# Rotated projection in eight products per chunk instead of twelve, with the two halves added by VectorE

## The reference, cut to what matters

```
ct_q  = x @ Wd_q_w + Wd_q_b
query = heads(ct_q @ Wu_q_w + Wu_q_b) + heads(rope(ct_q @ Wq_r_w + Wq_r_b))
ct_kv = x @ Wd_kv_w + Wd_kv_b
key   = heads(ct_kv @ Wu_k_w + Wu_k_b) + heads(rope(x @ Wk_r_w + Wk_r_b))
value = heads(ct_kv @ Wu_v_w + Wu_v_b)
```

## Time and profile before

| | |
|---|---|
| median of 3 runs | 3408.21 us |
| lowest and highest | 3405.76 and 3410.78 us |
| the profiled execution | 3409.91 us, its span 3408.1 us |
| projection, chunks 0 to 15 | from 69.94 us to about 687.6 us of the span |
| one chunk in the loop | 37.15 us |
| PE busy over the whole span | 94% |

### The profile page before, as it was taken

The page is one execution under the profiler, slowest core; times in us unless marked ns, Lnnn a source line. Parts: engine busy times, 40 slices in busy tenths (PEclk is TensorE's granted clock), DMA queues, the critical chain, the costliest instruction groups (busy, mean ns, idle before and its releaser), DMA issues. The chain is left out here.

```text
span 3408.1 us, 49590 instructions
## 1 busy us (share of the span) xinstructions
PE 3214.4 (94%) x16020; PEld 2024.3 (59%) x16020; DVE 2122.1 (62%) x2249; ACT 1538.2 (45%) x2714; POOL 2025.6 (59%) x654
## 2 busy tenths in 40 slices
PE   7999999989999999999999999999995999999998
PEld 4888888744444444444444444444442777877777
DVE  3545554756666666666666666666643778777774
ACT  1222221146666656566656666666663233232332
POOL 0111111157777777787777777877784566666653
PEclk8999999989999999999999999999997999999999
DMA  3544445544242423323242322324204223333230
GB/s 97 185 167 166 171 170 168 156 97 97 54 97 54 97 54 74 77 58 91 54 97 54 80 71 64 87 51 97 54 11 145 74 68 94 98 98 84 70 93 38
DMA packets 179890, 316.27 MB, mean 93 GB/s; under 512 B 16080, under 2 KB 52080, under 8 KB 179696
## 3 DMA queue, kind: packets, MB, share of 16 engines
q1 hardware_dynamic: 179696, 313.70, 33.4%
HBM read 194.59 MB, written 118.49 MB: 92 GB/s over the span
## 5 line engine op out<-in xcount | busy, mean ns | idle before, releaser
L275 DVE TENSOR_REDUCE row_max<-ps_m 128x1 f32<-128x1024 f32 x992 | 1156.2, 1220 | 635.9 <-PE ps_m L258 635.7
L912 POOL TENSOR_TENSOR pairs<-probs 128x2048 f32<-128x2048 f32 x256 | 1167.9, 4573 | 482.3 <-ACT probs L893 482.3
L893 ACT ACTIVATE probs<-ps_s 128x512 f32<-128x512 f32 x2048 | 1086.4, 599 | 539.5 <-PE ps_s L805 522.9
L258 PE MATMUL ps_m<-k_stack,q_stack 96*128 96x512 f32 x1984 | 871.1, 440 | 96.3 <-DVE row_max L275 41.8
L805 PE MATMUL ps_s<-q_stack,k_stack 97*128 97x512 f32 x2048 | 824.8, 406 | 6.2 <-PEq L306 4.1
L258 PEld LDWEIGHTS ps_m<-k_stack,q_stack 96*128 96x128 f32 x1984 | 379.0, 191 | 532.7 <-DVE row_max L275 391.0
L818 PE MATMUL ps_o<-probs,v_tiles 128*32 128x512 f32 x4096 | 502.6, 609 | 0.0
L805 PEld LDWEIGHTS ps_s<-q_stack,k_stack 97*128 97x128 f32 x2048 | 396.1, 194 | 88.4 <-ACT probs L893 20.0
L541 POOL TENSOR_TENSOR y_cos<-y_rot,cos 64x512 f32<-64x512 f32 x16 | 20.5, 1284 | 474.3 <-DVE y_swap L637 474.3
L916 POOL TENSOR_TENSOR pairs<-pairs 128x2048 f32<-128x2048 f32 x64 | 293.2, 4581 | 5.0
L818 PEld LDWEIGHTS ps_o<-probs,v_tiles 128*32 128x32 f32 x4096 | 108.3, 110 | 253.4 <-issue 195.4
(11 more groups left out here) (174 smaller groups left out, 4662.8 us busy)
## 6 DMA issues: line engine op xcount, KB each, us to landing
q_stack<-q_hi_scratch SPq DMA_DIRECT2D x128, 256.0 KB, 6.1
k_stack<-k_hi_scratch SPq DMA_DIRECT2D x64, 512.0 KB, 10.8
x_in<-in_x SPq DMA_DIRECT2D x16, 1024.0 KB, 5.6
q_hi_scratch<-st_hi SPq DMA_DIRECT2D x64, 256.0 KB, 2.3
q_lo_scratch<-st_lo SPq DMA_DIRECT2D x64, 256.0 KB, 2.5
k_hi_scratch<-st_hi SPq DMA_DIRECT2D x64, 256.0 KB, 2.4
k_lo_scratch<-st_lo SPq DMA_DIRECT2D x64, 256.0 KB, 2.7
v_scratch<-st_v SPq DMA_DIRECT2D x64, 256.0 KB, 2.3
```

The lines of the kernel that those rows point to most:

```text
L258: product = nc.tensor.matmul(slot[:, kc, :], att["q"][r][0:ROWS, half, h, q * P:(q + 1) * P], att["k"][r][0:ROWS, h, kc * CH:(kc + 1) * CH ...
L275: nc.vector.reduce_max(att["row_max"][:, half, j:j + 1], slot[:, :, :].rearrange("p k t -> p (k t)"), AX).then_inc(att["m_read"], 1)
L893: nc.scalar.activation(probs[:, (r * UNITS + u) % PR, x // HG, x % HG, :], ps_s[place(u * UT + x) % SR][:, :], ACT.Exp, scale=SCALE).then_ ...
L912: nc.gpsimd.tensor_tensor(pairs[:, w, :, :], probs[:, (r * UNITS + u) % PR, 0, :, :], probs[:, (r * UNITS + u) % PR, 1, :, :], ALU.add).th ...
```

## The change

Before, the high part of the 64 turned columns and their low part each had a weight tile of 128 columns with 64 columns of zeros. Now both lie in one tile `rot` of 128 columns: high in columns 0 to 63, low in columns 64 to 127. For each block f this tile is multiplied by high x and by low x, so 8 matmuls take the place of 12 (the product of low weight and low x comes in addition to what was computed before). Rows 0 to 63 of `ps_r` then hold what comes from the high weights, rows 64 to 127 what comes from the low ones. ACT copies rows 0 to 63 with the bias to `y_rot` as before; a new DVE instruction adds rows 64 to 127 to `y_rot` in place and sets the new semaphore `rot_full`. DVE itself waits for `rot_full` before the swap. PE waits for `rot_full` where it waited for `rot_y`: before the rotation of the following chunk, and in the last chunk before the first item. Two clearings of the zero columns are gone.

```diff
-                    nc.vector.tensor_tensor(w["rot_lo"][:, c, 0:HD], y[:, 0:HD], w["rot_hi"][:, c, 0:HD],
+                    nc.vector.tensor_tensor(w["rot"][:, c, 2 * HD:3 * HD], y[:, 0:HD], w["rot"][:, c, 0:HD],
                                             ALU.subtract).then_inc(lo_done, 1)
...
-            for part in ("rot_hi", "rot_lo"):
-                nc.vector.memset(w[part][:, :, 2 * HD:P].bitcast(F32), 0.0)
...
-            def rotated(c, par, between):
+            def rotated(c, par):
+
                 if not is_first(c):
-                    pe.wait_ge(rot_y, c)
-                features(ps_r[:, :], par, "rot", slice(0, P), between).then_inc(rot_proj, 1)
+                    pe.wait_ge(rot_full, c)
+                for f in range(FC):
+                    nc.tensor.matmul(ps_r[:, :], w["rot"][:, f, :], xT_hi[par][:, f, :], start=f == 0, stop=False)
+                    m = nc.tensor.matmul(ps_r[:, :], w["rot"][:, f, :], xT_lo[par][:, f, :], start=False, stop=f == FC - 1)
+                m.then_inc(rot_proj, 1)
...
-                    rotated(c, par, lambda: None)
+                    rotated(c, par)
                     if final:
-                        pe.wait_ge(rot_y, c + 1)
+                        pe.wait_ge(rot_full, c + 1)
...
                     dve.wait_ge(rot_y, c + 1)
+                    nc.vector.tensor_tensor(y_rot[:, :], ps_r[2 * HD:P, :], y_rot[:, :], ALU.add).then_inc(rot_full, 1)
                     if not is_first(c):
                         dve.wait_ge(rot_sum, c * 2)
+                    dve.wait_ge(rot_full, c + 1)
                     dve.sem_inc(held, 1)
                     nc.vector.stream_shuffle(y_swap[:, :], y_rot[:, :], SWAP).then_inc(rot_swap, 1)
```

More of the change, by code:

```diff
@@ L148, in _ @@
                     nc.scalar.copy(w["q_hi"][:, c, :], ps_a[i % 2][:, :])
-                    nc.scalar.copy(w["rot_hi"][:, c, 0:HD], ps_y[i % 2][:, 0:HD]).then_inc(hi_done, 1)
+                    nc.scalar.copy(w["rot"][:, c, 0:HD], ps_y[i % 2][:, 0:HD]).then_inc(hi_done, 1)
                 elif kind == 1:
@@ L152, in _ @@
                     nc.scalar.copy(w["k_hi"][:, c, :], k_full[:, c % 2, :])
-                    nc.scalar.copy(w["rot_hi"][:, c, HD:2 * HD], wkr[:, c, 0:HD]).then_inc(hi_done, 1)
+                    nc.scalar.copy(w["rot"][:, c, HD:2 * HD], wkr[:, c, 0:HD]).then_inc(hi_done, 1)
                 else:
@@ L186, in _ @@
                     nc.vector.tensor_tensor(w["k_lo"][:, c, :], kf, w["k_hi"][:, c, :], ALU.subtract)
-                    nc.vector.tensor_tensor(w["rot_lo"][:, c, HD:2 * HD], wkr[:, c, 0:HD], w["rot_hi"][:, c, HD:2 * HD],
+                    nc.vector.tensor_tensor(w["rot"][:, c, 3 * HD:P], wkr[:, c, 0:HD], w["rot"][:, c, HD:2 * HD],
                                             ALU.subtract).then_inc(lo_done, 1)
@@ L341, in project_block @@
         rot_y = sem("rot_y")
+        rot_full = sem("rot_full")
         rot_swap = sem("rot_swap")
@@ L1445, in block_program @@
             t["bv"] = sb("bv", [P, D])
-            w = {k: sb("w_" + k, [P, FC, D if len(k) == 4 else P], F32R)
-                 for k in ("q_hi", "q_lo", "k_hi", "k_lo", "v_hi", "v_lo", "rot_hi", "rot_lo")}
+            w = {k: sb("w_" + k, [P, FC, P if k == "rot" else D], F32R)
+                 for k in ("q_hi", "q_lo", "k_hi", "k_lo", "v_hi", "v_lo", "rot")}
             x_in = [sb(f"x_in{i}", [P, TPC, D]) for i in range(CPB)]
```

## The result

| | before | after |
|---|---|---|
| median of 5 runs | 3410.58 us | 3428.86 us |
| lowest and highest | 3405.76 and 3413.48 us | 3426.55 and 3430.16 us |
| span of the profiled execution | 3408.1 us | 3428.4 us |

The ratio is 1.0055, with a 95% interval from 1.004 to 1.0069: slower. The forecast was 3399.0 us, with a range of 3394 to 3404.

A forecast was written before the change was run, and what follows sets the result against it. PE's issue was taken to bound the projection. Saving 14.5 us, less stalls of 12 x 0.35, 3 x 0.13 and 0.73, gave 9.2 us: 3408.2 - 9.2 = 3399.0 us, range 3394 to 3404.

The forecast's parts named there:

- The saving: Projection's rotation on PE: four fewer matmuls per chunk at 0.227 us save 0.907 us, 14.5 us over 16 chunks.
- The add's price and D: New DVE add costs 0.69 us; D, the swap's delay against the rotation's end, is 0.67 us (0.58 to 0.79).
- The last chunk: PE's first item waits 0.73 us longer for `rot_full`, so this chunk gains only 0.18 us.
- The projection's sum: Saving less stalls over the projection's chunks: 14.5 - 12 x 0.35 - 3 x 0.13 - 0.73 = 9.2 us.
- my own formula: PE's stall before the transposes per loop chunk: D + 0.15 - 0.47 = D - 0.32, taken as 0.35 us.
- What is removed. Four matmuls of 512 columns per chunk: Sum's first term, in the projection: 64 executed matmuls at 0.227 us give 14.5 us.
- or if the time moves in attention, where nothing was changed: Listed sign that the forecast is wrong: time changes in unedited attention; no size or chance given.
- The rivals: Three alternatives: PE never waits, 3394.4 us (8%); new link eats the gain, 3404.2 (8%); pauses lower the clock, 3423 (4%).
- the clock rival: In the projection, new PE pauses lower the clock, losing 24 us against 9 gained: 3423 us; chance 4%.

The follow-up runs named there:

- Eight products alone: Kernel before without the rotation's third product (low weights by high x), without the add and without fillers: 3423.89 us, ratio 1.0042.
- the add alone: Kernel before, twelve products kept, plus the new DVE add, `rot_full` and its three waits: 3413.12 us against 3409.32, ratio 1.0011.
- 48, 20 and 12 fillers: Kernel after with 48, 20 or 12 counter increments nobody waits for, ahead of PE's first wait for weights: 3401.72, 3401.03 and 3403.58 us.
- 4 fillers: Kernel after with 4 counter increments nobody waits for, ahead of PE's first wait for weights: 3430.51 us, ratio 1.0064.
- eight products and 48 fillers: Kernel before without the rotation's third product and without the add, plus 48 unawaited counter increments ahead of PE's first wait: 3394.33 us, ratio 0.9953.

## Why the prediction was wrong

- **The saving** of 0.907 us per chunk, 14.5 in all: right. Eight products alone give a chunk of 36.240 us against 37.146.
- **The add's price and D**: right. 0.69 us in all 16 chunks; ACT ends at 330.16 and the mask is loaded at 331.04, so the tail is 0.88 us where I had 0.92 (old 0.25 + 0.67), D = 0.63. The loop chunk lost 0.35 us in the kernel after and 0.358 with the add alone. That it is 0.35 to the hundredth is partly luck: by my own formula D = 0.63 gives 0.31 us, and some 0.05 us went inside the transposes, which I had not priced (from the first of them to the next item 0.84 us instead of 0.79).
- **The last chunk**: right, 0.73 us.
- **The projection's sum**: forecast 9.2 us. From the first rotation to the last chunk's first item it took 553.33 us instead of 562.55, 9.2 us less. The agreement to a tenth is partly luck, since chunk 0 alone differs by more from trace to trace (38.83 us before, 37.97 after, 36.4 to 39.9 over all); chunks 1 to 14, which do not vary so, gained 8.16 us where the sum's terms give 8.24. With 48, 20 and 12 fillers, which put the loop's head off the edge, the kernel is 8.6, 9.3 and 5.6 us faster than the kernel before in the medians.
- **The step that failed** is the first of the sum, "What is removed. Four matmuls of 512 columns per chunk". It counted the matmuls that are executed and forgot those that are written; the effect of a shorter program stood in the sum at nothing, without a reason. 48 instructions left PE's program ahead of a loop of 2179 instructions, and its head, which had stood 38 behind an edge, came to stand 10 ahead of it. That cost 26.6 us in attention. I had even named the sign, "or if the time moves in attention, where nothing was changed", but as something that would make me wrong and not as a case with a price.
- **The rows were there.** The earlier trace rows show a pause of 2.76 us released by nobody at the head of a turn, and I used them as a price for the clock. The question to ask was what that pause is. It is eight times in the trace, with an instruction packet beside it, and whether a second one follows depends on where the loop lies.
- **The rivals.** None of the three happened. The clock did stay at 1.00 through the projection's new stalls. It was low for longer in attention, behind the second pause: a price like that of the clock rival was paid there, at most the 26.6 - 18.3 = 8.3 us over eight heads, by another cause and at another place.
- **What stays open.** The last stage is 1.4 us longer in the kernel after (797.0 against 795.6). Its loop's head also came to lie close ahead of an edge, but its jumps back bring no instruction packet, before and after, so the edge has nothing to act on there. The other traces have 795.1 to 797.2 us there (795.9 with 4 fillers, 796.4 with eight products and 48 fillers), so 1.4 us is within the spread. How much of attention's 8.3 us beside the pauses is the clock is open, as said above. What the edge costs at distances between 10 and 56 instructions ahead was not tried. From the 2.6 to 3.5 us at which a second pause ends and the 0.235 us per matmul there, an estimate is that 15 matmuls between head and edge would do.

## What to carry to other kernels

An edit that takes instructions out of, or puts them into, one engine's program moves all that follows it. Where a hardware loop comes later, count the instructions by which it moves, look whether the instruction queue has packets while the loop turns (here it had for 2179 instructions and not for 860), and look at each turn's first instructions for a pause with no releaser. Where two pauses stood instead of one, 12 idle instructions ahead of the loop, in a place where the engine waits anyway, gave back some 24 us here and 20 of them some 28, each kernel set against the kernel before of its own session. When a change has a good sum in its own stage and a bad total, cut both spans at the same marks before looking for a cause in the edited code. And a link that is put into a loop of hand-overs (here copy, add, swap, POOL, norm, transposes) is priced by the lead at its end; to take work out of that loop, as the norm's statistics here, gave back some 5 us more (9.3 us faster than the kernel before became 14.1).

## What the runs showed of the hardware

- An instruction packet carries 16.4 KB, 256 instructions. In a loop of 2179 instructions PE stood for 2.7 to 3.3 us at each jump back. If the next edge lies 6 or 10 instructions behind the head, it stood another 1.7 to 3.0 us. The packet of the next piece started only 0.4 to 1.0 us behind the turn's first matmul; with 56 instructions (21 matmuls) to the edge that was soon enough. The Trainium skill (Runtime: NRT & Kernel Launch, section Instruction fetch mechanics) calls the crossing of a block's edge mostly hidden; right behind a jump it is not here.
- PE loops of 709 to 725 and of 860 instructions fetched nothing from their second turn on and had no such pause; the loop of 2179 brought 10 packets from one jump back to the next in the kernel before and 11 in the kernel after (counted in the trace from 1052 to 1229 us and from 1044 to 1224 us).
- A counter increment on PE that nobody waits for takes 0.156 us: with 162 and 208 of them the first matmul starts at 25.55 and 32.72 us. 48 of them moved it only from 7.59 to 8.13 us, since PE waited for the weights until 7.6 us anyway.
- DVE's normalising of four tiles takes 1.91 us alone and 4.89 us beside POOL's products, and DVE's 128x4 add 0.17 us with POOL quiet and 1.18 us behind a POOL add. What is moved off a chain can become slower by its new neighbour.
